# Weighing the values with the turned probabilities as the moving operand, in quarters of the array

## What is computed

```
scores = q k^T                      # 16 heads, 256 x 256 each
probs  = exp(scores - max)          # entries below the row's threshold become 0
out    = (probs v) / sum(kept probs)
y      = out Wo + bo
```

## Time and profile before

| what | value |
|---|---|
| runs (3) | median 2046.71 us, 2041.70 to 2064.53 us |
| the profiled execution | 2043.58 us |
| its span, first to last instruction | 2041.8 us |
| TensorE, VectorE, ScalarE busy over the span | 80%, 72%, 55% |
| granted TensorE clock, mean over the span | 0.791 of 2.4 GHz |
| second attention: from the first to the last weighing | 592 to 1105 us |

### The profile page before, as it was taken

The page is one execution under the profiler, slowest core; times in us unless marked ns, Lnnn a source line. Parts: engine busy times, 40 slices in busy tenths (PEclk is TensorE's granted clock), DMA queues, the critical chain, the costliest instruction groups (busy, mean ns, idle before and its releaser), DMA issues.

```text
span 2041.8 us, 38862 instructions
## 1 busy us (share of the span) xinstructions
PE 1642.0 (80%) x12640; PEld 1172.7 (57%) x12640; DVE 1476.3 (72%) x4747; ACT 1115.7 (55%) x3322; POOL 877.4 (43%) x1162
## 2 busy tenths in 40 slices
PE   3888989897358988988779978527777799999978
PEld 3445667675236766766668645413443477777763
DVE  6678776555588988999887842358876777887657
ACT  2444444445988898899852423214452366666620
POOL 3333221124253554444433577676300377767610
PEclk8889999997555555555557989858896899999969
DMA  4111101003000000000001023322110000000000
GB/s 139 47 47 41 40 21 42 18 2 122 15 9 17 12 13 11 17 9 9 1 1 59 23 78 110 97 65 73 48 72 20 15 1 1 2 1 2 1 1 21
DMA packets 67305, 67.58 MB, mean 33 GB/s; under 512 B 9955, under 2 KB 58966, under 8 KB 66566
## 3 DMA queue, kind: packets, MB, share of 16 engines
q1 hardware_dynamic: 58930, 53.09, 7.9%
q0 software_dynamic: 5120, 10.50, 2.0%
q10 hardware_dynamic: 3040, 1.38, 0.2%
HBM read 30.41 MB, written 8.39 MB: 19 GB/s over the span
## 4 chain that ended last, share of the span: by engine, by line
PE 35%; DVE 27%; ACT 12%; issue 10%; POOL 6%; SPq 6%; ACTq 2%; DMA 1%; DVEq 0%; POOLq 0%
SPq L689 5%; POOL weights L1165 4%; DVE weights L3212 3%; PE bank L2143 3%; PE bank L1551 3%; PE bank L2103 3%; ACT big L4445 3%; PE bank L1567 3%; DVE weights L3156 3%; DVE nmax L3072 2%; DVE small L3200 2%; PE bank L1758 2%; PE bank L2130 2%; ACT rope_s L4235 2%; ACT rope_c L4235 2%
## 5 line engine op out<-in xcount | busy, mean ns | idle before, releaser
L1758 PEld LDWEIGHTS bank<-V,probsT 128*128 128x128 f32 x1024 | 203.6, 297 | 28.4 <-ACT probsT L4246 13.7
L1758 PE MATMUL bank<-V,probsT 128*128 128x9 f32 x1024 | 205.4, 333 | 15.2 <-ACT probsT L4246 10.9
L2711 DVE TENSOR_REDUCE nmax<-bank 128x4 f32<-128x1024 f32 x144 | 175.9, 1221 | 51.8 <-PE bank L1331 48.8
L891 POOL TENSOR_TENSOR big<-big,rinv 128x512 f32<-128x512 f32 x128 | 131.7, 1049 | 45.7 <-DVE rinv L3767 45.7
L1745 PE MATMUL bank<-silu_b,weights 128*128 128x128 bf16 x464 | 138.9, 303 | 0.0
L4050 ACT ACTIVATE feat_o<-bank 128x1024 f32<-128x1024 f32 x72 | 73.7, 1023 | 101.5 <-PE bank L1331 66.7
L4050 ACT ACTIVATE O<-bank 128x1024 f32<-128x1024 f32 x72 | 73.7, 1024 | 97.2 <-PE bank L1331 70.6
L3761 DVE TENSOR_REDUCE nmax<-bank 128x2 f32<-128x512 f32 x128 | 81.9, 682 | 58.1 <-PE bank L2103 58.1
L4445 ACT ACTIVATE big<-bank,nmax 128x256 f32<-128x256 f32 x256 | 117.6, 478 | 11.1 <-DVE nmax L3761 11.1
L4453 ACT ACTIVATE big<-bank 128x512 f32<-128x512 f32 x128 | 73.8, 614 | 68.8 <-PE bank L2130 68.8
L4246 ACT ACTIVATE probsT<-bank 128x512 f32<-128x512 f32 x128 | 75.9, 600 | 58.4 <-PE bank L1745 39.0
(11 more groups left out here) (818 smaller groups left out, 5110.5 us busy)
## 6 DMA issues: line engine op xcount, KB each, us to landing
qT<-parts SPq DMA_DIRECT2D x276, 32.0 KB
big<-V SPq DMA_DIRECT2D x192, 32.0 KB
y_rows<-weights SPq DMA_DIRECT2D x24, 256.0 KB, 2.3
big<-parts SPq DMA_DIRECT2D x180, 32.0 KB
weights<-in_weights_l_ffn SPq DMA_DIRECT2D x1, 4832.0 KB, 14.3
weights<-in_weights_l_attn SPq DMA_DIRECT2D x1, 3904.0 KB, 13.0
qT<-V SPq DMA_DIRECT2D x96, 32.0 KB
weights<-in_weights_l_ffn SPq DMA_DIRECT2D x1, 2860.0 KB, 11.7
```

Source lines behind the costliest of these rows:

```text
L891: nc.gpsimd.tensor_tensor(row, row, rinv[:, h % H, :].unsqueeze(2).to_broadcast([P, T, S]), ALU.mult).then_inc(scaled.sem, 1)
L1758: last = mm(pb[1][:, t * S + h * wide:t * S + (h + 1) * wide], probsT[:, h % 2, at:at + P], values_of(b, k)[:, h * wide:(h + 1) * wide], s ...
L2711: V_.tensor_reduce(to, scored.rearrange("p (i a n) -> p i a n", i=HPG, n=n), AX.X, ALU.max, negate=True).then_inc(score_max.sem, 1)
```

## The change

1. `l1_weigh` swaps the operands. The stationary operand is now the nine columns of values and ones (128 by 9), the moving one the head's turned probabilities for all 256 queries (two products, one for each half of the keys, in place of four). Head h writes to the nine partitions from 32 (h mod 4) of the first 256 columns of bank 1: four heads stand below one another in the four quarters, with features on the partitions and queries in the columns.
2. After four heads ScalarE copies these columns to SBUF (`l1_take_quad`), and TensorE turns them back (`l1_turn_quad`): for each query tile a product of the copy (128 by 128, stationary) with the identity's 36 columns that belong to the four heads. Heads 0 to 11 land in the second half of bank 1, heads 12 to 15 in its first 72 columns. That is 4 copies and 8 products for each element.
3. `weighed` reads from the two places, so that its first and last instruction become two each; it waits for the last turning back.
4. The weighing of head 12 stands behind the turning of head 14 and the second last turning back of the element (heads 8 to 11) (before: ahead of the turning of head 14), as the quarter's bank columns must be copied first.
5. The semaphores of the third layer's feed-forward part (l2_ffn) are renamed and shared (`side_psum`, `side_taken`); what waits for what is as before there.

```diff
-                wide = HD + 1
-                for t in range(T):
-                    for k in range(T):
-                        at = t * S + k * P
-                        last = mm(pb[1][:, t * S + h * wide:t * S + (h + 1) * wide], probsT[:, h % 2, at:at + P],
-                                  values_of(b, k)[:, h * wide:(h + 1) * wide], start=k == 0, stop=k == T - 1)
+                wide, part = HD + 1, slice(32 * (h % 4), 32 * (h % 4) + HD + 1)
+                by_keys = probsT[:, h % 2, :].rearrange("p (t k n) -> p k t n", t=T, k=T)
+                for k in range(T):
+                    last = mm(pb[1][part, 0:S].rearrange("p (t n) -> p t n", t=T), values_of(b, k)[:, h * wide:(h + 1) * wide], by_keys[:, k],
+                              start=k == 0, stop=k == T - 1)
                 last.then_inc(pv_done.sem, 1)
+
+            def l1_turn_quad(b, q, ph="l1_attn"):
+                pe.wait_ge(side_taken.sem, side_taken(ph, b, q + 1))
+                of_heads = C("ident").rearrange("p (j d) -> p j d", j=4)[:, :, 0:HD + 1]
+                heads_there, there = weighed_at[q // 3]
+                at = 4 * q - heads_there.start
+                for t in range(T):
+                    o = there.rearrange("p (t h d) -> p t h d", t=T, d=HD + 1)[:, t, at:at + 4, :]
+                    last = mm(o, weighed_quad[:, t * P:(t + 1) * P], of_heads, start=True, stop=True)
+                last.then_inc(side_psum.sem, 1)
...
+                    if now(n - 1):
+                        l1_turn_quad(n - 1, QUADS - 1)
...
                     if now(n):
+                        l1_turn_quad(n, 0)
                         l1_weigh(n, 4)
...
                         l1_turn_probs(n, 10)
+                        l1_turn_quad(n, 1)
                         l1_weigh(n, 8)
...
                         l1_weigh(n, 11)
+                        l1_turn_probs(n, 14)
+                        l1_turn_quad(n, 2)
                         l1_weigh(n, 12)
-                        l1_turn_probs(n, 14)
                         l1_turn_probs(n, 15)
...
             def weighed(b, ph="l1_attn"):
-                dve.wait_ge(pv_done.sem, pv_done(ph, b, H))
+                dve.wait_ge(side_psum.sem, side_psum(ph, b, QUADS))
...
-                link(V_.scalar_tensor_tensor(kept_sum, sums_by_tile, 1e-10, o1[:, :, :, HD], ALU.mult, ALU.add))
+                for of, there in weighed_at:
+                    o1 = there.rearrange("p (t h d) -> p t h d", t=T, d=HD + 1)
+                    link(V_.scalar_tensor_tensor(kept_sum[:, :, of], sums_by_tile[:, :, of], 1e-10, o1[:, :, :, HD], ALU.mult, ALU.add))
...
+            def l1_take_quad(b, q, ph="l1_attn"):
+                act.wait_ge(pv_done.sem, pv_done(ph, b, 4 * q + 4))
+                nc.scalar.activation(weighed_quad, pb[1][:, 0:S], ACT.Copy).then_inc(side_taken.sem, 1)
...
                     if now(n):
+                        l1_take_quad(n, 2)
                         l1_take_probs(n, 14)
```

More of the change, by code:

```diff
@@ L59 @@
 GROUP_WORDS = 4 * S // 2
+QUADS = H // 4
 QUICK_STEPS = 3
@@ L475, in adaln_program @@
         minus_two = silu_b[:, 0:P // 2].bitcast(BF16)
+        weighed_quad = V[:, 0, 576:576 + S]
+        early_heads = 3 * H // 4
+        weighed_at = ((slice(0, early_heads), pb[1][:, S:S + T * early_heads * (HD + 1)]),
+                      (slice(early_heads, H), pb[1][:, 0:T * (H - early_heads) * (HD + 1)]))
         first_rows = front_n[:].rearrange("p t d -> p (t d)")
@@ L606, in adaln_program @@
         ranks_psum = wide_signal("ranks_psum", l1_ffn=3, l2_ffn=2 * PAIRS)
-        z_psum = signal("z_psum", l2_ffn=1)
-        z_ready = signal("z_ready", l2_ffn=1)
+        side_psum = signal("side_psum", l1_attn=QUADS, l2_ffn=1)
+        side_taken = signal("side_taken", l1_attn=QUADS, l2_ffn=1)
         rope_ready = signal("rope_ready", l3_attn=2 * NQ3)
@@ L1883, in l1_attn @@
                         l1_weigh(n, 15)
+                l1_turn_quad(B - 1, QUADS - 1)
                 l1_turn_out(B - 1)
@@ L2059, in l2_fall @@
                     last = mm(pb[6][:], W(ph, "win2")[:, c * P:(c + 1) * P], gelus(c), start=c == 0, stop=c == O2 - 1)
-                last.then_inc(z_psum.sem, 1)
+                last.then_inc(side_psum.sem, 1)
             def l2_out(p, ph="l2_ffn"):
                 pe.wait_ge(pass_done.sem, pass_done(ph, p, 1))
-                pe.wait_ge(z_ready.sem, z_ready(ph, p, 1))
+                pe.wait_ge(side_taken.sem, side_taken(ph, p, 1))
                 for j in range(2 * T):
@@ L3225, in weighed @@
                 linkup()
-                V_.tensor_tensor(tokens1.rearrange("p t (h d) -> p t h d", h=H), o1[:, :, :, 0:HD],
-                                 kept_sum.unsqueeze(3).to_broadcast([P, T, H, HD]), ALU.mult).then_inc(tok_ready.sem, 1)
+                for of, there in weighed_at:
+                    o1 = there.rearrange("p (t h d) -> p t h d", t=T, d=HD + 1)
+                    heads_there = of.stop - of.start
+                    last = V_.tensor_tensor(tokens1.rearrange("p t (h d) -> p t h d", h=H)[:, :, of], o1[:, :, :, 0:HD],
+                                            kept_sum[:, :, of].unsqueeze(3).to_broadcast([P, T, heads_there, HD]), ALU.mult)
+                    if of.stop == H:
+                        last.then_inc(tok_ready.sem, 1)
+                    else:
+                        link(last)
             def l1_result(b, ph="l1_attn"):
@@ L3728, in l2_ffn @@
                                    ranks_z[:, 2 * following:2 * following + 2, :]).then_inc(pair_ready.sem, 1)
[L3729 removed]
+                dve.wait_ge(side_psum.sem, side_psum(ph, p, 1))
                 two = lambda v: v.rearrange("p (r k) -> p r k", r=2)
                 V_.scalar_tensor_tensor(two(pair_rank2), two(pb[6][R2:2 * R2, :]), W(ph, "win2b")[R2:2 * R2, :],
[L3732 removed]
+                                        ranks_gate[R2:2 * R2, 2 * p:2 * p + 2, :], ALU.add, ALU.mult).then_inc(side_taken.sem, 1)
                 dve.wait_ge(out_psum.sem, out_psum(ph, p, 1))
@@ L4257, in l1_attn @@
                         l1_count(n + 1, 0, 20, 21)
+                    if now(n - 1):
+                        l1_take_quad(n - 1, QUADS - 1)
                     if now(n + 3):
@@ L4295, in l1_attn @@
                     if now(n):
+                        l1_take_quad(n, 0)
                         l1_take_probs(n, 5)
@@ L4313, in l1_attn @@
                     if now(n):
+                        l1_take_quad(n, 1)
                         l1_take_probs(n, 9)
@@ L4347, in l1_attn @@
                         l1_count(n + 2, 0, 17, 20)
+                l1_take_quad(B - 1, QUADS - 1)
                 l1_take_out(B - 1)
@@ L4424, in l2_ffn @@
             def l2_ffn(p, ph="l2_ffn"):
-                act.wait_ge(z_psum.sem, z_psum(ph, p, 0))
+                act.wait_ge(side_psum.sem, side_psum(ph, p, 0))
                 for c in range(O2):
```

4 lines of the change are left out of this document (1 added, 3 removed).

## The result

| kernel | median | runs | lowest to highest |
|---|---|---|---|
| before | 2053.42 us | 13 | 2041.70 to 2064.53 us |
| changed | 2071.38 us | 13 | 2065.11 to 2078.11 us |

The ratio is 1.0103 (95% interval 1.0083 to 1.0124): the change makes the kernel 1.0% slower. The profiled execution of the changed kernel took 2071.47 us with a span of 2069.7 us, 27.9 us more than the span of before. The profiled execution of before, from which the prediction's sum was made, lies 10 us under the median of its 13 runs; between the medians the difference is 18 us.

What follows compares the result with a forecast made beforehand. VectorE was taken to bound the step. On the profiled 2043.58 us: six step ends +1.2, VectorE +1.6, the end -1.4, low-clock ends +5.2, together +6.6: 2050.2, taken as 2050 us; range 2033 to 2070.

Steps and rivals of the forecast that it cites:

- VectorE bounds the step: Second attention's 71.1 us step: VectorE's 64.56 busy, 3.87 branch, 0.97 wait for the doubts and 1.7 small pauses.
- The weighing at equal clock: Weighing a head on TensorE: 1.70 us at 1.2 GHz or 0.85 at 2.4, nothing gained at equal clock.
- 0.2 more: VectorE's `weighed`, with one more product of each kind: 0.2 us more an element, 8 x 0.2 = 1.6 us.
- The clock rises: Second attention: TensorE's clock expected at 2.4 GHz in most of the turnings and weighings.
- The last element: End of the second attention: VectorE's 1.72 us wait goes, less 0.3 us for copy and turning back: -1.4 us.
- ScalarE's counting becomes the bound: Rival, chance 0.22: each ScalarE copy paid in full, 7 steps x 1.05 + 1.6 = +9 us, 2053 us.
- The step end: Ends of elements 0 to 5: six x 0.2 = +1.2 us, plus 2 x 2.6 = +5.2 for ends at 1.2 GHz.
- the path to the doubts, laid out again at 2.4 GHz: Step end, ScalarE's copy to the doubts: ready at 794.8 where the sum stood at 794.88, taken as +0.2 us.
- one end in three: Step ends taken to be still at 1.2 GHz: 2 x 2.6 = +5.2 us.
- its upper bound: Step end with the whole chain at 1.2 GHz: doubts at 797.6, 2.8 us later.
- the slower rival: Clock stays where it was, chance 0.17: six step ends x 2.8 = 17 us, +21 in all, 2065 us.
- the 3.7 laid out: Step end at 2.4 GHz: chain from the copy's landing at 791.11 to head 15 weighed by 794.8.

Runs made afterwards that it cites:

- the filler experiment: Changed kernel plus 28 idle products on TensorE between the turning of head 14 and the turning back of heads 8 to 11: 2064.78 us, ratio 1.0083.
- the form without the trip: Changed kernel without the four copies and eight products that turn heads back, heads 12 and 14 in the old order: 2036.89 us, ratio 0.9941.
- The third buffer: Changed kernel with three buffers for the turned probabilities instead of two, the copy staying late: 2058.82 us, ratio 1.0036.
- the copy early: Changed kernel with ScalarE's copy of heads 8 to 11 moved behind the exponentials of head 13, ahead of l1_start: 2038.2 us, ratio 0.9956.

## Why the prediction was wrong

**VectorE bounds the step: right.** Its busy time stayed (64.60 for 64.56 us), so did the branch, and all forms that took the wait for the doubts away came out at 69.8 to 70.6 us in the step that is shown here, whatever TensorE or ScalarE did.

**The weighing at equal clock: right.** Four passes take 1.81 us at clock 0.50 (797.26 to 799.07), where 1.70 was worked out, and 0.96 at 1.00 (794.40 to 795.36 in the filler experiment), where 0.85 was worked out. Heads 13 and 14 do run side by side: at clock 1.00 the row of 8 passes is 1.04 us long and that of 4 is 1.03. `weighed`, from its first instruction to the next one behind it, grew from 0.94 to 1.08 us; 0.2 more had been taken.

**The clock rises: right, in the mean.** 0.54 became 0.75 between 600 and 1000 us. It is the swapped weighing that does it: the form without the trip has 0.79 there, and the old weighing with its heads reordered 0.53.

**The last element: right.** 1.2 us shorter in the profiled executions, forecast 1.4.

**ScalarE's counting becomes the bound: no.** ScalarE's copies cost 1.3 us of its time a step (1.05 was worked out), beside its waits. It became the limit in another way, by the place of one of them in its queue.

**The step end: wrong, and this is 18 of the 21 us by which the sum is off.** The step that failed is "the path to the doubts, laid out again at 2.4 GHz", with its result of +0.2 us and six times that in the sum. Measured in the step shown: 75.63 us where there were 70.82 (724.28 to 795.10), +4.8. It comes from:

- The clock of the chain. I let one end in three be at 1.2 GHz, "as the clock falls back while TensorE waits for VectorE at a step's start". It is every one, and the wait that does it isn't the one at the start: it is the 7.6 us which the change itself creates, ahead of the chain. The filler experiment puts it at 2.7 us a step. The chain's price at the low clock, +2.8, stood in the prediction, as its upper bound and as the slower rival; that rival had the wrong condition, since it was tied to the clock of the whole stage.
- The buffers. In the layout head 14 was moved at no time of its own: I had "head 12 weighed by 792.45; head 15 turned; moved; weighed" and did not ask when ScalarE may move head 14. Before, head 12 was weighed by 786.16, well ahead of 790.72. Now it is weighed inside the chain, and the two-buffer rule, which had stopped ScalarE for 1.1 us in all between 592 and 1045 us, stops it for 32.3 (before, then changed). The third buffer puts it at 1.5 us a step end.

```profile
ACT probsT L4246 <- PE bank L1758: 1.1, 2, 0.5
```

```profile
ACT probsT L4273 <- PE bank L1762: 32.3, 16, 3.0
```

- ScalarE's place in the chain came 0.8 us later in the step (790.72 - 724.28 = 66.4 before, 795.84 - 728.56 = 67.3 now). Ahead of it VectorE had waited once more for TensorE, for scores; it does so in two of the steps, 1.6 us in all, and why is not shown:

```profile
778.33 1.29 DVE L3092 TENSOR_REDUCE nmax<-bank 128x2 f32<-128x512 f32 x2 [0.73 <-PE bank L1734]
```

The first two make 4.2 us, beside the 4.3 by which the chain of 8.0 us exceeds the 3.7 laid out; they need not add up exactly, as each was taken away alone. What is shown is that the copy's place is upstream of both: moved, it removes the idle time, the low clock behind it, and the late weighing of head 12 at once.

The sum of the prediction with the measured size: the waits for the doubts grew by 29.8 - 5.4 = 24.4 us, 4 us in each of six step ends, where the sum had +6.4. With that it gives 2043.58 + 24.4 + 1.6 - 1.4 = 2068.2. The remaining 3.3 us to the profiled execution are the stretches ahead of and behind the stage (+2.3, which the traces' scatter covers), the rest of the seven steps (+2.3 for 1.6) and the last element (-1.2 for -1.4).

**The range.** 2070 as its upper end took 17 us for all step ends at the low clock and nothing for a wait that had not been thought of. Its base was low too: the profiled execution's 2043.58 us is 3 us under the median of the three runs shown, and 10 under that of the thirteen. (The lower end's -7.5 us takes the whole 1.72 us of the last element, where the sum takes 1.4.)

## What to carry to other kernels

When an operand is swapped so that a result must pass through another engine and back, the question isn't what the copy costs (0.38 us here) but what stands ahead of it in that engine's list, and what the first engine does meanwhile: the same instruction 8 us earlier in the step was the difference between 1.0% slower and 0.4% faster. When an operation is moved behind another, list each buffer that it frees; a rule such as "two buffers" that had hardly shown a wait (1.1 us) becomes a link of the chain (32.3). And price a chain behind an idle TensorE by rows at the low clock, whatever the mean clock of its stage: here all six chains behind 6 to 7.6 us of idle time ran at it.

## What was not expected of the hardware

Matmuls with nine stationary columns, a fourteenth of the array, and 256 moving ones raised the stage's clock from 0.54 to 0.75, and to 0.80 with the copy early. Two heads in neighbouring quarters take the time of one (1.04 us for 8 passes and 1.03 for 4 at 2.4 GHz). Entering and leaving the quarters for each of 16 heads shows no price on the path, as without the trip VectorE waits 0.2 us in all for the doubts: the Trainium skill, "TensorEngine Tiling (Array Packing)", "Key Properties", says that such a change drains TensorE, and no run here separates that; the changes lie beside VectorE's work.
